# A dense step with another order on every engine, and a second normalised tile that a DMA turns instead of TensorE

## The reference, cut to what matters

```
x = x + cross_attention(layernorm(x), ctx)        # 16 heads of 32, causal mask over 64 keys
n = layernorm(x)
logits = n @ router.T                             # 8 experts, the two largest logits are the weights
out = x + shared_expert(n) + sum over the two experts of logit * expert_e(n)
expert(n) = (silu(n @ wg) * (n @ wu)) @ wd        # inner width 256
```

## Time and profile before

| what | before |
|---|---|
| median of 3 runs (lowest, highest) | 845.55 us (842.5, 845.84) |
| the profiled execution, its span | 844.62 us, 842.9 us |
| PE busy, share of the span | 787.6 us, 93% |
| DVE | 607.5 us, 72% |
| ACT | 439.8 us, 52% |
| POOL | 428.1 us, 51% |
| granted clock of TensorE over the span | 0.976 |

### The profile page before, as it was taken

One profiled execution on the slowest core, in us unless ns is written; L12 is line 12 of the kernel. 1 busy time (PEld: TensorE's weight loads), 2 busy tenths in 40 slices (PEclk: granted clock), 3 DMA queues, 4 the chain that ended last, 5 costly groups with the idle time before them and its releaser, 6 DMA issues.

```text
span 842.9 us, 22260 instructions
## 1 busy us (share of the span) xinstructions
PE 787.6 (93%) x7500; PEld 545.4 (65%) x7500; DVE 607.5 (72%) x1196; ACT 439.8 (52%) x805; POOL 428.1 (51%) x530
## 2 busy tenths in 40 slices
PE   4668999999999999989999999999999999999994
PEld 1356777878887888867787877545555555545551
DVE  3878989999999999884468877555555555555552
ACT  2366777777878787866434633333333333333330
POOL 1133876667676767744400010375555666556543
PEclk9679999999999999999999999999999999999997
DMA  8304364635363634255665564698989999889892
GB/s 313 123 27 172 115 211 127 210 125 227 108 233 112 228 106 159 89 158 191 209 211 174 184 224 144 116 165 143 155 144 136 167 143 159 152 146 154 142 146 38
DMA packets 102760, 132.39 MB, mean 157 GB/s; under 512 B 54368, under 2 KB 55392, under 8 KB 101280
## 3 DMA queue, kind: packets, MB, share of 16 engines
q1 hardware_dynamic: 86784, 95.74, 38.5%
q0 software_dynamic: 15904, 35.70, 24.5%
HBM read 71.61 MB, written 52.31 MB: 147 GB/s over the span
## 4 chain that ended last, share of the span: by engine, by line
PE 57%; DVE 10%; issue 6%; DMA 3%; ACT 2%; POOL 2%; SPq 1%; DVEq 0%; POOLq 0%; ACTq 0%
PE psum L1279 38%; PE psum L1327 11%; PE psum L1270 5%; DMA hidT<-xn2T_f 2%; DVE head_max L1007 1%; DVE xy L1020 1%; DVE probsT L860 1%; DVE stats L924 1%; DMA normed_turned<-xn2T 1%; PE psum L1379 1%; DVE xn1T L860 1%; ACT attnT L698 1%; ACT probsT L698 1%; POOL rstd L532 1%; DMA out<-w_q,tabs 1%
## 5 line engine op out<-in xcount | busy, mean ns | idle before, releaser
L678 POOL DMA_INDIRECT out<-w_q,tabs x71 | 112.4, 1584 | 108.6 <-DVE w_q L1259 74.5
L668 POOL DMA_INDIRECT x_in<-normed_tokens,tabs x71 | 70.2, 989 | 132.5 <-DVE tabs L1145 83.9
L1244 DVE SCALAR_TENSOR_TENSOR hid<-psum,tabs,silu_g 128x256 f32<-128x256 f32 x71 | 34.3, 484 | 110.6 <-ACT silu_g L822 109.0
L822 ACT ACTIVATE silu_g<-psum,tabs 128x256 f32<-128x256 f32 x71 | 33.6, 473 | 145.3 <-PE psum L1279 139.1
L1279 PE MATMUL psum<-exp_all,hidT 128*128 x426 | 103.5, 379 | 3.1 <-DMA hidT<-xn2T_f 3.1
L1327 PE MATMUL psum<-xn1T,w_q 128*128 128x128 f16 x1536 | 94.5, 223 | 7.3 <-DVE xn1T L860 7.3
L1279 PE MATMUL psum<-exp_all,probsT 128*128 x420 | 96.4, 379 | 0.0
L1327 PEld LDWEIGHTS psum<-xn1T,w_q 128*128 128x128 f16 x1536 | 89.7, 100 | 7.9 <-DVE xn1T L860 7.6
L1279 PE MATMUL psum<-w_o,attnT 128*128 128x512 f16 x384 | 88.1, 379 | 0.2
L1279 PEld LDWEIGHTS psum<-exp_all,hidT 128*128 128x128 f16 x426 | 41.7, 98 | 54.0 <-issue 5.3
L1259 DVE TENSOR_SCALAR w_q<-psum,y_w 128x512 f32<-128x512 f32 x71 | 53.3, 751 | 21.5 <-PE psum L1279 15.3
(11 more groups left out here) (199 smaller groups left out, 1706.2 us busy)
## 6 DMA issues: line engine op xcount, KB each, us to landing
x_in<-x SPq DMA_DIRECT2D x64, 256.0 KB, 3.1
exp_all<-experts SPq DMA_DIRECT2D x8, 1536.0 KB, 8.5
out<-xy SPq DMA_DIRECT2D x32, 256.0 KB, 2.1
normed_tokens<-xn SPq DMA_DIRECT2D x32, 256.0 KB, 2.4
normed_turned<-xn2T SPq DMA_DIRECT2D x32, 256.0 KB, 2.0
w_q<-out SPq DMA_DIRECT2D x32, 256.0 KB, 3.2
out<-w_q SPq DMA_DIRECT2D x32, 256.0 KB, 2.9
probsT<-normed_turned SPq DMA_DIRECT2D x16, 256.0 KB, 3.4
```

Of the source, the lines that this page charges most:

```text
L668: pool.indirect_dma_start(x_in[:, t % 4, :], None, xn_dram, bass.IndirectOffsetOnAxis(gather_at[:, t:t + 1], 0)).then_inc(gathered[t % 4], 16)
L678: pool.indirect_dma_start(out, bass.IndirectOffsetOnAxis(add_at[:, t:t + 1], 0), y[:, t % Y_RING, :], None, bounds_check=TOKENS - 1, oob_i ...
```

## The change

What it does:
- **Second tile.** `rstd` of layernorm 2 carries the factor X_UP. ACT writes `xn2`, then `xn2p` high (a copy from SBUF to float16), POOL the rest; one transposing DMA of SP turns both parts (128x1024 float16) into `xn2T`. PE's four transposes and the two ACT copies of them go. SP stores `xn2T` at the start of the next step, after a wait for the turning. The router product stands behind the scores and ahead of the projection, and ACT's `logits` behind `xn1`. Gathered tiles carry the factor too, so their two operations in the routed stage have none.
- **Dense order.** On DVE a step begins with `qT`, then `join_stats(1)` of the step before, then the statistics; the magnitudes stand ahead of `head_max`; `recip` and `attn` come ahead of `xy`. On ACT `xn2` and `xn2p` stand behind `xn1T`, then come `xn1`, `logits`, pieces and the exponential. POOL's order stays, but for the weights.
- **Fill.** W_o and the router join the first scales, W_q is split first and in halves, the values in four parts spread over steps 0 to 3, the first turning moves to the front, and the scales of the shared expert come in steps 4 and 5. ACT and POOL split W_o and the shared expert piece by piece (POOL right behind `inv_std(0)`).
- **Experts.** Loaded at j=2 and one batch later, the magnitudes' way through DRAM is in two calls of SP; the last expert's pieces are split in entries 10 to 15 of the shared stage. Twelve steps are written out in place of eight.

The diff, cut to its core:

```diff
-            e = found(b - 2 if j == 0 else b - 1)
+            e = found(b - 3 if j == 0 else b - 2)
...
+                if live(t6):
+                    sp.wait_ge(xn2_turned, 16 * (t6 + 1))
+                    sp.dma_start(xT_dram[bass.ds(t6 * P, P), :], xn2T[:, :, :, :].rearrange("p v c q -> p (v c q)")
+                                 ).then_inc(xT_stored, 16)
...
-                e = found(b + 1)
-                if j == 0 and isinstance(b, int) and b == 2:
+                e = found(b)
+                if j == 0 and found(b - 2) is not None:
+                    from_dram(b - 2)
...
-                if j == 0 and e is not None:
-                    sp.wait_ge(expert_in, 16 * e)
+                    sp.wait_ge(v_split, VALUE_PARTS)
+                if j == 2 and e is not None:
+                    wait(sp, expert_in, 16 * e)
                     load_expert(e)
+                if j == 3 and found(b - 1) is not None:
+                    to_dram(b - 1)
...
-                    sp.wait_ge(xn2T_ready, t5 + 1)
-                    sp.dma_start(xT_dram[bass.ds(t5 * P, P), :], xn2T[:, :, :, :].rearrange("p v c q -> p (v c q)")
-                                 ).then_inc(xT_stored, 16)
-                if j == 3 and found(b) is not None:
-                    through_dram(b)
+                    sp.wait_ge(xn2_parts, t5 + 1)
+                    wait(sp, router_mm, t5)
+                    wait(sp, xT_stored, 16 * t5)
+                    plain(sp)
+                    sp.dma_start_transpose(xn2T[:, :, :, :].rearrange("p v c q -> p (v c) q"),
+                                           xn2p[:, :, :].rearrange("p v h -> p (v h)")).then_inc(xn2_turned, 16)
...
-            load_expert(0)
...
-                pool.tensor_scalar(rstd[:, which, 0:1], moments[:, which, 1:2], EPS, None, ALU.add).then_inc(ln_eps[which], 1)
+                pool.tensor_scalar(rstd[:, which, 0:1], moments[:, which, 1:2], EPS, (1.0, X_UP ** -2)[which], ALU.add,
+                                   ALU.mult).then_inc(ln_eps[which], 1)
...
-                if tile in (2, 3):
-                    pool.wait_ge(wo_scaled, 2)
-                    for k in range(2 * tile - 4, 2 * tile - 2):
+                if tile in (3, 4):
+                    for k in range(2 * tile - 6, 2 * tile - 4):
+                        pool.wait_ge(wo_scaled, 2 * (k + 1))
                         low_weights(w_o, wo_raw, k * PIECE, PIECE, wo_split)
                 if tile == 4:
-                    pool.wait_ge(wsh_scaled, 6)
+                    pool.wait_ge(wsh_scaled, 2)
                     low_weights(w_r, r_raw, 0, C * E, wsh_split)
-                if tile in (5, 6, 7):
-                    for k in range(2 * tile - 10, 2 * tile - 8):
+                if tile in (7, 8, 9):
+                    for k in range(2 * tile - 14, 2 * tile - 12):
+                        pool.wait_ge(wsh_scaled, 2 * (k + 2))
                         low_weights(w_sh, sh_raw, k * PIECE, PIECE, wsh_split)
...
+                if isinstance(tile, int):
+                    more_weights(tile)
...
-                    pool.wait_ge(xn2T_hi, 2 * (t5 + 1))
+                    pool.wait_ge(xn2_hi, t5 + 1)
                     if j == 3:
                         wait(pool, v_bd_ready, 2 * (b + 1) if live(t3) else 0)
                     plain(pool)
-                    pool.tensor_tensor(flat(xn2T[:, 1, :, :]), xn2T_f[:, :], flat(xn2T[:, 0, :, :]),
-                                       ALU.subtract).then_inc(xn2T_ready, 1)
+                    pool.tensor_tensor(xn2p[:, 1, :], xn2[:, (j + 1) % 2, 0:H], xn2p[:, 0, :],
+                                       ALU.subtract).then_inc(xn2_parts, 1)
...
+            for k in range(PIECES):
+                low_piece(E - 1, k)
...
+            def more_weights(tile):
+                if tile in (2, 3):
+                    act.wait_ge(scales_ready, 2)
+                    for k in (2 * tile - 4, 2 * tile - 3):
+                        weight_piece(w_o, wo_raw, k * PIECE, PIECE, M_WO, wo_scaled)
+                if tile == 3:
+                    weight_piece(w_r, r_raw, 0, C * E, M_R, wsh_scaled)
+                if tile in (6, 7, 8):
+                    act.wait_ge(scales_ready, 3)
+                    for k in (2 * tile - 12, 2 * tile - 11):
+                        weight_piece(w_sh, sh_raw, k * PIECE, PIECE, M_GU if k < GU // PIECE else M_DOWN, wsh_scaled)
...
-                if live(t6):
-                    act.wait_ge(router_mm, t6 + 1)
-                    copy(logits[:, bass.ds(t6, 1), :], psum[:, 6, 0:E], sc[:, S_R:S_R + 1], logits_ready)
-                if live(t5):
-                    act.wait_ge(ln_rstd[1], t5 + 1)
-                    wait(act, xn2_stored[(j + 1) % 2], 16 * (TPB // 2 * b + (j - 5) // 2))
-                    act.activation(xn2[:, (j + 1) % 2, 0:H], x1, ACT.Identity, bias=rstd[:, 1, 2:3],
-                                   scale=rstd[:, 1, 1:2]).then_inc(xn2_ready, 1)
...
                 if live(t5):
-                    act.wait_ge(xn2T_mm, t5 + 1)
-                    wait(act, xT_stored, 16 * t5)
-                    copy(flat(xn2T[:, 0, :, :]), bank(6), X_UP, xn2T_hi)
-                if live(t5):
-                    wait(act, xn2T_ready, t5)
-                    copy(xn2T_f[:, :], bank(6), X_UP, xn2T_hi)
-                if isinstance(b, int) and (b, j) == (0, 2):
-                    more_weights()
-                if isinstance(b, int) and (b, j) == (0, 3):
-                    shared_weights()
+                    act.wait_ge(ln_rstd[1], t5 + 1)
+                    wait(act, xn2_stored[(j + 1) % 2], 16 * (TPB // 2 * b + (j - 5) // 2))
+                    act.activation(xn2[:, (j + 1) % 2, 0:H], x1, ACT.Identity, bias=rstd[:, 1, 2:3],
+                                   scale=rstd[:, 1, 1:2]).then_inc(xn2_ready, 1)
+                    act.wait_ge(xn2_ready, t5 + 1)
+                    wait(act, xn2_turned, 16 * t5)
+                    copy(xn2p[:, 0, :], xn2[:, (j + 1) % 2, 0:H], 1.0, xn2_hi)
                 if live(tile):
                     act.wait_ge(ln_rstd[0], tile + 1)
                     act.activation(xn1[:, :], x_in[:, j % 2, 0:H], ACT.Identity, bias=rstd[:, 0, 2:3],
                                    scale=rstd[:, 0, 1:2]).then_inc(xn1_ready, 1)
+                if isinstance(t2, int) and t2 == 0:
+                    high_values(2)
+                if isinstance(tile, int):
+                    more_weights(tile)
+                if live(t6):
+                    act.wait_ge(router_mm, t6 + 1)
+                    copy(logits[:, bass.ds(t6, 1), :], psum[:, 6, 0:E], sc[:, S_R:S_R + 1], logits_ready)
...
+                        if ROUTE_AT <= n < ROUTE_AT + PIECES:
+                            high_piece(E - 1, n - ROUTE_AT)
...
-                t1, t2, t3, t4 = [tile - n for n in range(1, 5)]
-                e = found(b)
-                scaled = found(b - 1) if j == 1 else None
+                t1, t2, t3, t4, t5 = [tile - n for n in range(1, 6)]
+                e = found(b - 1)
+                scaled = found(b - 2) if j == 1 else None
+                if live(t2):
+                    dve.wait_ge(qT_hi, t2 + 1)
+                    low(flat(qT[:, 1, :, :]), bank(5), Q_DOWN, flat(qT[:, 0, :, :]), qT_ready)
+                if live(t5):
+                    join_stats(1, t5)
                 if live(tile):
                     dve.wait_ge(xa_loaded[j % 2], 16 * (TPB // 2 * b + j // 2 + 1))
                     stage_stats(0, x_in[:, j % 2, 0:H], tile)
-                if live(tile):
-                    join_stats(0, tile)
-                if live(t2):
-                    dve.wait_ge(qT_hi, t2 + 1)
-                    low(flat(qT[:, 1, :, :]), bank(5), Q_DOWN, flat(qT[:, 0, :, :]), qT_ready)
-                if e is not None and j in ((1, 2, 3) if isinstance(b, int) and b == 0 else (0, 2, 3)):
-                    expert_magnitudes(e, max(0, j - 1))
-                if scaled is not None:
-                    expert_scales(scaled, 0)
                 if live(t4):
                     dve.wait_ge(attnT_hi, t4 + 1)
                     dve.tensor_tensor(flat(attnT[:, 1, :, :]), bank(4), flat(attnT[:, 0, :, :]),
                                       ALU.subtract).then_inc(attnT_ready, 1)
+                if live(tile):
+                    join_stats(0, tile)
                 if scaled is not None:
-                    expert_scales(scaled, 1)
+                    expert_scales(scaled, 0)
                 if live(t3):
                     for n in range(2):
                         dve.wait_ge(probsT_hi, 2 * t3 + n + 1)
                         low(probsT_flat[:, 8 * P + 4 * P * n:8 * P + 4 * P * n + 4 * P], bank(n), P_UP,
                             probsT_flat[:, 4 * P * n:4 * P * n + 4 * P], probsT_ready)
                 if scaled is not None:
+                    expert_scales(scaled, 1)
+                if live(t1) and not (isinstance(t1, int) and t1 == 0):
```

(53 more changed lines are left out.)

240 lines of the change are left out of this document (139 added, 101 removed).

## The result

The changed kernel takes **877.26 us** (median of 4 runs, 875.44 to 881.45); the kernel before, run beside it, 844.02 (839.87 to 845.84). The ratio is 1.041, 95% interval 1.035 to 1.047: slower by about 33 us, as forecast in sign, 12 us above the point and inside the range. The profiled execution spans 879.4 us where the one before spanned 842.9; it is the slowest of the four (881.45), so this difference of 36.5 us is 3 us more than that of the medians.

The account below looks back on a forecast made before the run. DVE and PE nearly fill the 40.90 us batch, but a chain through ACT and POOL was to bind the changed loop. 844.62 - 2.8 (fill) + 28 (loop) + 0 = 869.8, less issue gaps: 865 us, range 830 to 880.

Parts of the forecast that it names:

- The chain: Dense loop: the late join delays POOL's work, ACT's xn1, pieces and qT; batch 46.0 us for 40.9, +28 us in all.
- the walk: Dense step followed from DVE's qT with the old profile's durations; steps of 11.9, 10.7, 10.7 and 12.7 us.
- gaps of issue that a chain counts twice: Deduction from the sum for steps with pieces: 0.3 us a step over some 17 steps, bringing 869.8 to 865.
- The fill: Start up to tile 8: earlier first product, less deferred work and new waits; -2.8 us (-9 to +2).
- The waits blamed: Fill: POOL's weight splits ahead of batch_values, W_o's last pieces, PE waiting for second magnitudes; new waits 15.0 us, +5.6.
- Everything else: PE's fewer transposes, drain, last expert's pieces, ACT's saving and routed stage, together counted at 0 (-2 to +4).
- the count, ended at step 32: Dense loss added from step 10 to the last scores: five batches +25.5, two steps +3.0, step 32 -0.5.
- The turning DMA: SP's transpose of xn2: 2.4 us of issue, issued at 7.9, landing near 11.8, hidden in steps of 10.7 and more.
- Rival 1: Dense loop: DVE stays the bound and the new order pays; 828 to 834, said 831 us; chance 0.21.
- Rival 2: Dense loop: only ACT's in-order rest binds, batch 41.9, 848 us (843 to 854); chance 0.10.
- Rival 3: Turned tile lands late behind an expert's load and PE waits; 852 us, or up to 872; chance 0.08 alone.
- The test stated for rival 1: Dense loop: it decides from the point where xn1 starts within 5 us of DVE's qT in every step.

Follow-up runs that it names:

- a_join: The changed kernel with join_stats(1) back at the end of its own DVE step, right behind stage_stats(1); 849.3 us, ratio 1.006.
- a_inter: The changed kernel with DVE's qT moved behind the three statistics calls; 845.4 us, ratio 1.005.
- a_two: The changed kernel with a second piece buffer, so ACT's second piece does not wait for POOL's rest of the first; 869.3 us, ratio 1.029.
- a_pieces: The changed kernel with POOL's second rest of a step moved behind inv_std(0) of the next step; 871.2 us, ratio 1.034.
- best2: best1 with POOL's second rest also behind inv_std(0), batch_values and xn2p's rest of the next step; 831.2 us, ratio 0.985 to the kernel before.
- a_xn2: The changed kernel with ACT's xn2 right behind its qT again, ahead of the copies; 923.7 us, ratio 1.095.
- a_fill: The changed kernel with POOL's rests of the weights behind batch_values and xn2p's rest; 877.3 us, ratio 1.044.
- a_head: a_join with the statistics of x_in and join 0 also ahead of DVE's qT, as in the kernel before; 845.7 us, ratio 1.001.
- b_turn: The kernel before with the turning DMA alone, router product behind the scores; 847.0 us, ratio 1.004.
- best1: a_inter with two piece buffers and POOL's rests of the weights behind batch_values; 836.1 us, ratio 0.991 to the kernel before.
- b_join: The kernel before with only join_stats(1) moved behind qT of the next DVE step; 933.4 us, ratio 1.105.

## Why the prediction was right, step by step

**The chain, right in mechanism and in size.** Against the steps foretold for j=0, 1, 2, 3 (11.9, 10.7, 10.7, 12.7) the trace has 11.86, 10.60, 10.67 and 12.42. Inside j=0 the marks fall where the walk put them: `xn1` at 6.1 (foretold 6.2), the exponential at 8.2 (8.5), ACT's second piece at 10.0 (10.0), DVE's `qT` at 11.9 (11.9). In j=3 POOL's rest of the first piece starts at 9.2 (9.4). The loop lost 26.2 us from tile 8 to tile 31 for 28 foretold. Of these 2.6 us are two steps j=3 at a lower clock, which no term of the sum had, so the waits alone are nearer 24. a_join and a_inter show the cause: moving one of DVE's short calls gives 28 or 30 us back. The 4.8 us taken off the sum for "gaps of issue that a chain counts twice" had no ground in the trace: the sum without it, 869.8, was nearer, and what it left out is below, in the fill and the drain.

**What the walk left out.** In j=3 it named one way through POOL, the pieces. a_two and a_pieces show a second, `batch_values` and `av`, of nearly the same length. It did not change the forecast, but it is the likely reason why each single cure was worth about half of what the expectations said. That best2 needed all of its parts is not shown: they were not taken out one by one. The walk also passed over `xn2`'s new place on ACT without a price; a_xn2 puts 46 us on it.

**The fill, right in parts, low in its waits.** Tile 0 came at 34.94 (foretold 38.2), a gain of 17.9 for 14.7. DVE's work up to tile 8 is 80.60 for 79.55 foretold. DVE's idle time is 100.47 - 80.60 = 19.9 us for 15.0 foretold. Together -0.1 at tile 8 for -2.8. The waits blamed are there: up to tile 8 PE stood 4.6 us for `batch_values`, 3.4 for W_o's rests and 4.2 for the second magnitudes. It also stood 2.8 us for the turned tile, which the forecast did not have. But the place of `qT` ahead of the three statistics calls costs more, 8.7 us by a_inter, against 3.9 for POOL's rests by a_fill's trace. It is not the late join alone: a_join, with the join back and the statistics of `x_in` still behind `qT`, has tile 8 at 135.8, and only a_head, with these ahead of `qT` too, at 130.1. DVE's waits in that stretch of the kernel after:

```profile
DVE recip L1080 <- PE psum L1474: 8.9, 3, 3.8
DVE qT L905 <- ACT qT L729: 5.2, 5, 2.4
```

**Everything else: the step that failed.** It was put at 0 (-2 to +4), and the trace has +10.3: 6.2 in drain and shared stage, 4.1 in the routed stage. The first is the same join once more (a_join takes 145.9 us there for 152.5), in a place that the count, ended at step 32, passed over. In the drain the entries of the shared stage stand on DVE between a step's end and the next step's head, so the join waits for them too, and for what they wait for. The chain of waits of the kernel after:

```profile
421.99 1.17 POOL xn2p L630
423.25 3.29 SPq L440
426.59 3.36 DMA w_q<-out
...
430.72 0.18 DVE moments L988
...
431.39 0.56 POOL rstd L559
```

The load of a base (`w_q<-out`) is queued on SP behind the turning DMA, and DVE's entry waits 0.55 us for it. The last join comes at 430.72, 2.8 us behind the end of its statistics and 33.7 us after `head_max` of tile 31; in a_join it comes 28.9 us after it. From tile 31 to the first gathered tile the kernels that join in their own step (before, a_join, a_head, b_turn) take 144.2 to 146.3 us, the ten that join in the next one 147.6 to 154.4, a_inter, best1 and best2 among them: this is left in the best kernel. The second, 4.1 us, is no effect of the change as far as these traces tell: a_xn2 and best1 have the changed routed code and take 325.3 and 325.1 us there, the kernel before 325.8, and the others lie between 325.0 and 329.9.

**The turning DMA.** Its issue is 1.24 us where 2.4 was taken; it doubles the bytes of the DMA in the earlier trace rows and costs SP 0.05 us more. It lands 3.1 us after issue (foretold 3.9; no row stood behind its doubled issue and its 1.5 us of transfer), at the latest 7.6. In the loop it is hidden, as forecast, but for 1.4 us in batch 3; in the fill it is not, PE stood 1.9 and 0.8 us for it there. The Trainium skill's Advanced Engine Details and Errata (X-Bar Transpose) says that TRN2 transpose DMAs are as fast as regular ones; by that rule, the trace agrees within 0.4 us on the landing: the store of the same 256 KB lands in 2.7 us. Its issue holds SP longer, 1.24 us for the store's 0.36.

**The rivals.** Rival 1 was wrong here for the reason given against it, and right as a goal: 831 us was its time, and best2 has a median of 831.2, which is in part luck: tile 8 came 12.2 us earlier than before where rival 1 had 2.8 to 9, and the drain lost 2.1. Rival 2 is nearest to a_join, a batch of 41.6 for 41.9. Rival 3 appears in most batches of b_turn alone (0.9 to 1.7 us); in the loops of the changed kernel, a_join, a_head and best1 it comes once, 1.0 to 1.5 us. The test stated for rival 1 tells only half: `xn1` starts 3.7 to 4.0 us behind DVE's `qT` in the settled steps of best2 and 4.9 to 6.1 in the kernel after, but a_head keeps it within 4.5 us in every one and still takes 41.8 a batch. An early `xn1` is needed, and is not enough.

## What to carry to other kernels

On engines that work in order, price a moved call not by its own duration but by everything queued behind its result on the next engines: here 0.17 us of `bn_aggr` put behind a wait for ACT held 5.4 us of POOL's work and cost 28 us. Before moving a producer later, look at where each in-order consumer stands: the late join cost 28 us with `xn2` behind the copies (a_join) and 90 with it ahead of them (b_join). And when a cure gives half of what it should, look for a second way of nearly the same length before dropping the theory: here the second buffer and POOL's order gave 8 and 6 us, each by itself; a batch bound by DVE alone was seen only with both and the earlier statistics.
